# Rounding of the FFN weights moved to GpSimd, and a new order for the last two token tiles

## The reference

```python
x = x + xattn(layernorm(x), ctx, Wq, Wk, Wv, Wo)     # 16 heads of 96, 4 key/value heads, softmax in f32
x = x + ffn(layernorm(x), w_gate, w_up, w_down)      # inner width 2752

def fake_quant(t, axis):
    s = jnp.maximum(jnp.max(jnp.abs(t), axis=axis, keepdims=True) / 127.0, 1e-08)
    return jnp.clip(jnp.round(t / s), -128.0, 127.0) * s
def qlinear(x, w):                                   # per row of x, per row of w
    return jnp.einsum('bsh,oh->bso', fake_quant(x, -1), fake_quant(w, 1))
h = silu(qlinear(x, w_gate)) * qlinear(x, w_up);  out = qlinear(h, w_down)
```

## Time and profile before

| what | us |
|---|---|
| time of three runs, median (lowest to highest) | 1581.5 (1580.5 to 1582.52) |
| the profiled execution: its own time, its span | 1579.16, 1577.5 |
| busy in the span: PE, DVE, ACT, POOL | 1500.4, 1104.9, 635.1, 649.6 |
| PE's mean granted clock, share of full speed | 0.991 |

### The profile page before, as it was taken

The page is one execution under the profiler, slowest core; times in us unless marked ns, Lnnn a source line. Parts: engine busy times, 40 slices in busy tenths (PEclk is TensorE's granted clock), DMA queues, the critical chain, the costliest instruction groups (busy, mean ns, idle before and its releaser), DMA issues.

```text
span 1577.5 us, 23750 instructions
## 1 busy us (share of the span) xinstructions
PE 1500.4 (95%) x7985; PEld 747.4 (47%) x7985; DVE 1104.9 (70%) x2012; ACT 635.1 (40%) x1164; POOL 649.6 (41%) x845
## 2 busy tenths in 40 slices
PE   5999989999998999999899999979899999999997
PEld 2544445554443555444465544434444444444443
DVE  5355664666686567768576666773899999999984
ACT  4356555555454545546455545551211111111110
POOL 4187775554667654557654556671000000000000
PEclk9999999999999999999999999999999999999998
DMA  7299999879999987899998999999934233332332
GB/s 241 79 256 220 245 241 213 183 180 241 283 275 201 221 197 160 220 296 247 225 201 199 229 253 267 234 212 263 307 96 110 65 95 99 85 96 78 85 96 58
DMA packets 487084, 297.82 MB, mean 189 GB/s; under 512 B 405789, under 2 KB 443985, under 8 KB 485841
## 3 DMA queue, kind: packets, MB, share of 16 engines
q1 hardware_dynamic: 486993, 296.68, 76.0%
HBM read 143.13 MB, written 46.69 MB: 120 GB/s over the span
## 4 chain that ended last, share of the span: by engine, by line
PE 74%; SPq 8%; DMA 7%; DVE 4%; issue 2%; POOL 2%; ACT 2%; DVEq 0%; ACTq 0%
PE ps_s L1570 17%; PE ps_g L1603 10%; PE ps_g L935 10%; PE ps_g L937 10%; PE ps_g L936 10%; PE ps_s L1031 7%; SPq L807 4%; PE ps_o L1047 3%; PE ps_o L1048 3%; DMA pT<-p_nat 3%; PE ps_o L1050 2%; SPq L787 1%; DMA xnT<-xh 1%; POOL p_nat L910 1%; PE ps_s L1032 1%
## 5 line engine op out<-in xcount | busy, mean ns | idle before, releaser
L910 POOL TENSOR_TENSOR p_nat<-p_f,p_nat 128x512 f16<-128x512 f32 x256 | 309.4, 1209 | 140.8 <-ACT p_nat L1147 140.3
L905 POOL TENSOR_SCALAR p_f<-p_f,small 128x576 f32<-128x576 f32 x256 | 201.8, 788 | 273.9 <-DVE small L1261 272.9
L1136 ACT ACTIVATE p_f<-ps_s,small 128x576 f32<-128x576 f32 x256 | 188.6, 737 | 257.4 <-DVE small L1256 252.7
L1256 DVE TENSOR_REDUCE small<-ps_s 128x1 f32<-128x576 f32 x256 | 191.4, 748 | 101.8 <-PE ps_s L1032 100.7
L1031 PE MATMUL ps_s<-k,q 96*128 96x512 f16 x768 | 224.6, 382 | 22.2 <-ACT p_f L1136 19.1
L1570 PE MATMUL ps_s<-w_gu_sb,xT 128*128 128x512 bf16 (+1 forms) x1152 | 226.5, 357 | 5.4 <-DVE g_sb L1690 4.1
L1623 ACT ACTIVATE g_sb<-g_sb,sx 128x512 f32<-128x512 f32 (+1 forms) x128 | 74.5, 582 | 381.1 <-DVE g_sb L1690 331.6
L1147 ACT ACTIVATE p_nat<-p_f 128x576 f16<-128x576 f32 x256 | 172.7, 676 | 111.2 <-POOL p_f L905 60.6
L1555 POOL TENSOR_TENSOR rstd<-var_eps,minus_half 128x1 f32<-128x1 f32 x16 | 8.8, 548 | 425.1 <-DVE var_eps L1645 425.1
L1603 PE MATMUL ps_g<-w_dn_sb,hT 128*128 128x512 bf16 x704 | 162.4, 384 | 6.1 <-DMA hT<-h_int 5.3
L1570 PEld LDWEIGHTS ps_s<-w_gu_sb,xT 128*128 128x128 bf16 x1152 | 112.3, 98 | 117.2 <-DVE g_sb L1690 8.8
(11 more groups left out here) (114 smaller groups left out, 2465.9 us busy)
## 6 DMA issues: line engine op xcount, KB each, us to landing
w_in<-w_gu SPq DMA_DIRECT2D x40, 512.0 KB, 4.8
wq<-wq_c SPq DMA_DIRECT2D x36, 512.0 KB, 4.8
wo<-wo_c SPq DMA_DIRECT2D x24, 768.0 KB, 6.2
gu_q<-w_t SPq DMA_DIRECT2D x44, 256.0 KB, 4.7
w_in<-w_dn SPq DMA_DIRECT2D x8, 1376.0 KB, 7.1
x_acc<-x SPq DMA_DIRECT2D x4, 2048.0 KB, 9.0
x<-x_acc SPq DMA_DIRECT2D x8, 1024.0 KB, 6.0
x_ln<-x SPq DMA_DIRECT2D x16, 512.0 KB, 3.6
```

The costliest lines, as they stand in the source:

```text
L905: nc.gpsimd.tensor_scalar(f, f, inv_sum[:, j % 2, t:t + 1], P_UP, ALU.mult, ALU.mult).then_inc(p_scaled, 1)
L910: nc.gpsimd.tensor_tensor(h[:, S + C:2 * S], f[:, 0:T], h[:, 0:T], ALU.subtract)
L1136: nc.scalar.activation(p_f[:, tile(b, j, t) % NF, :], scores(t), ACT.Exp, bias=neg_max[:, j % 2, t:t + 1], accum_out=sums[:, j % 2, t:t + ...
L1256: nc.vector.tensor_reduce(neg_max[:, j % 2, t:t + 1], scores(t), AX.X, ALU.max, negate=True).then_inc(mx_done, 1)
```

## The change

`round` goes from DVE's stream to POOL's, with the same waits and the same due time; `turn` stays on DVE. POOL's planned order is otherwise that of before. In the FFN, `x_quant` of the next tile runs before the two products of quarter 2 instead of behind the quarter's maximum. The last tiles are written out: PE runs gates(14), the first half of down(13), gates(15), the second half of down(13), down(14), down(15). The transposed x of tile 15 goes to `xT0`, the transposed h of tiles 14 and 15 to two buffers in the part of `w_first` that held the first quarter's gate weights (free after the third group of gates(15)), and the residual of tile 14 to `x_ln`. down(15) has three pieces of 512, 256 and 256 columns, each with a bank, a result and a store of its own.

```diff
@@ stage_events
-            dve += [(t, "round", g, h), (t + 2.5, "turn", g, h)]
+            pool.append((t, "round", g, h))
+            dve.append((t + 2.5, "turn", g, h))
@@ gpsimd (the same function is removed from vector, where it waited on dve)
+        def round_off(g, h):
+            n = ITEM["w", g]
+            rows, cols = unit_part(g, h)
+            pool.wait_ge(w_up, lifts(g, h))
+            pool.wait_ge(w_turned, TURNS.index((g, h)))
+            nc.gpsimd.tensor_scalar(w_int[0:rows, 0:cols.stop - cols.start], slot_of(n)[0:rows, cols], MAGIC, None,
+                                    ALU.subtract).then_inc(w_out, 1)
@@ ffn_phase
+    hT_last = [w_first[:, i * IC * P:(i + 1) * IC * P].rearrange("p (c n) -> p c n", c=IC) for i in range(2)]
+    LAST = TILES - 1
+    PIECES_OUT = ((0, 512), (512, 256), (768, 256))
@@ x_transpose
+            other = isinstance(t, int) and t in (0, LAST)
+            if other and t:
+                sp.wait_ge(gu_done, NUSE)
+            elif not first:
                 sp.wait_ge(gu_done, t * NUSE)
...
+            sp.dma_start_transpose((xT0 if other else xT)[:], x_int[:]).then_inc(x_turned, EV)
@@ h_transpose(t, last=None)
             sp.wait_ge(h_q, t + 1)
+            if last is None:
+                sp.wait_ge(d_done, t * 2)
+            else:
+                sp.wait_ge(gu_done, LAST * NUSE + QU)
@@ sync
-        x_transpose(TILES - 1)
-        for t in (TILES - 2, TILES - 1):
-            h_transpose(t)
-            store(t - 1)
-            res_tile(t)
-        store(TILES - 1)
+        x_transpose(LAST)
+        h_transpose(LAST - 1, 0)
+        res_before_last()
+        h_transpose(LAST, 1)
+        store(LAST - 2)
+        res_tile(LAST, LAST - 1)
+        store(LAST - 1, x_ln)
+        store_last()
@@ tensor
+        def down_last():
+            pe.wait_ge(h_turned, TILES * EV)
+            for i, (a, n) in enumerate(PIECES_OUT):
+                if i < 2:
+                    pe.wait_ge(d_read, LAST * 2 + (i + 1))
+                for c in range(IC):
+                    rows = P if c < IC - 1 else I_LAST
+                    mm = nc.tensor.matmul(kept.ps_g[i][:, 0:n], hT_last[1][0:rows, c, :],
...
+                mm.then_inc(d_done, 1)
...
-        with pe.Fori(0, TILES - 2) as t:
+        with pe.Fori(0, TILES - 4) as t:
             gates(t + 2)
             down(t + 1)
-        down(TILES - 1)
+        gates(LAST - 1)
+        down(LAST - 2, halves=(0,))
+        gates(LAST, xT0)
+        down(LAST - 2, halves=(1,))
+        down(LAST - 1, False, hT_last[0])
+        down_last()
@@ vector, gates
                 gate_piece(t, q, 0)
                 gate_piece(t, q, 1)
+                if nxt is not None and q == 2:
+                    x_quant(nxt, turned)
                 product(t, q, 0)
                 product(t, q, 1)
                 quarter_max(t, q)
@@ vector, the end
+        gates(LAST - 1, LAST, LAST * EV)
+        h_part(LAST - 1, LAST * EV - EV)
+        next_x_scale()
+        result(LAST - 2, (0,))
+        gates(LAST)
+        h_part(LAST, LAST * EV, sh_last)
+        result(LAST - 2, (1,))
         next_h_scale()
+        result(LAST - 1, x_res=x_ln)
+        result_last()
```

More of the change, by code:

```diff
@@ L336, in stage_events @@
         done[n] = t
-    return act, dve, sp
+    return act, dve, pool, sp
 def token_events(b):
@@ L911, in chances_lo @@
             nc.gpsimd.tensor_tensor(h[:, S:S + C], f[:, T:S], h[:, T:S], ALU.subtract).then_inc(p_low, 1)
-        run = {"power": power, "tokens_lo": tokens_lo, "context_lo": context_lo, "scaled": chances_scaled, "low": chances_lo,
+        def round_off(g, h):
[5 more added lines that the diff above has]
+                                    ALU.subtract).then_inc(w_out, 1)
+        run = {"round": round_off, "power": power, "tokens_lo": tokens_lo, "context_lo": context_lo, "scaled": chances_scaled, "low": chances_lo,
                **ffn["gpsimd"](pool)}
@@ L1291, in tile_scale @@
             nc.vector.reciprocal(w_inv[0:rows, :], s).then_inc(w_small, 1)
[L1293 to L1300, removed]
         def turn(g, h):
@@ L1327, in vector @@
         run = {"split": w_split, "stats": norm_stats, "norm": norm_tokens, "evac": evac, "max": row_max,
-               "invert": invert, "out_lo": out_lo, "scale": tile_scale, "round": round_off, "turn": turn, "add": add_out,
+               "invert": invert, "out_lo": out_lo, "scale": tile_scale, "turn": turn, "add": add_out,
                **ffn["vector"](dve)}
@@ L1474, in x_transpose @@
             sp.nop(nofuse=True)
-            sp.dma_start_transpose((xT0 if first and t == 0 else xT)[:], x_int[:]).then_inc(x_turned, EV)
+            sp.dma_start_transpose((xT0 if other else xT)[:], x_int[:]).then_inc(x_turned, EV)
         def load_gates(q, i):
@@ L1514, in sync, with store, res_before_last, store_last @@
         ln_tile, res_tile, x_transpose = steps["ln_tile"], steps["res_tile"], steps["x_transpose"]
-        def store(t):
+        def store(t, res=x_res):
             sp.wait_ge(r_done, t * 2 + 4)
-            sp.dma_start(out[bass.ds(t * P, P), :], x_res[:]).then_inc(out_s, EV)
-        def h_transpose(t):
+            sp.dma_start(out[bass.ds(t * P, P), :], res[:]).then_inc(out_s, EV)
+        def res_before_last():
+            sp.wait_ge(x_q, TILES + 1)
+            sp.dma_start(x_ln[:], x2[(LAST - 1) * P:LAST * P, :]).then_inc(res_in, EV)
+        def store_last():
+            for i, (a, n) in enumerate(PIECES_OUT):
+                c = slice(a, a + n)
+                sp.wait_ge(r_done, LAST * 2 + 3 + i)
+                sp.dma_start(out[LAST * P:TILES * P, c], x_res[:, c]).then_inc(out_s, EV)
+        def h_transpose(t, last=None):
             sp.wait_ge(h_q, t + 1)
-            sp.wait_ge(d_done, t * 2)
+            if last is None:
+                sp.wait_ge(d_done, t * 2)
+            else:
+                sp.wait_ge(gu_done, LAST * NUSE + QU)
             sp.nop(nofuse=True)
-            sp.dma_start_transpose(hT[:], h_int[:]).then_inc(h_turned, EV)
+            sp.dma_start_transpose((hT if last is None else hT_last[last])[:], h_int[:]).then_inc(h_turned, EV)
         def load_down(q):
@@ L1587, in tensor, with gates, down @@
         first_gate = tensor_steps(pe)
-        def gates(t):
+        def gates(t, x=xT):
             pe.wait_ge(x_turned, t * EV + EV)
             for n in range(NUSE):
-                gate_group(pe, t, n, xT)
-        def down(t, first=False):
+                gate_group(pe, t, n, x)
+        def down_last():
+            pe.wait_ge(h_turned, TILES * EV)
+            for i, (a, n) in enumerate(PIECES_OUT):
+                if i < 2:
[3 more added lines that the diff above has]
+                    mm = nc.tensor.matmul(kept.ps_g[i][:, 0:n], hT_last[1][0:rows, c, :],
+                                          w_dn[0:rows, c // KC, a // 32:(a + n) // 32,
+                                               c % KC * 32:(c % KC + 1) * 32],
+                                          start=(c == 0), stop=(c == IC - 1))
+                mm.then_inc(d_done, 1)
+        def down(t, first=False, hT=hT, halves=(0, 1)):
             pe.wait_ge(h_turned, t * EV + EV)
-            for h in range(2):
+            for h in halves:
                 pe.wait_ge(d_read, t * 2 + (h + 1))
@@ L1691, in gate_piece @@
                 dve.wait_ge(gu_done, t * NUSE + (n + 2))
-                if q == 0 and not (isinstance(t, int) and t == 0):
+                if q == 0 and isinstance(t, int) and t == LAST:
+                    dve.wait_ge(r_done, t * 2 - 1)
+                elif q == 0 and not (isinstance(t, int) and t == 0):
                     dve.wait_ge(r_done, t * 2)
@@ L1732, in gates, with h_part @@
                         x_norm(nxt)
-                    elif q == 2:
-                        x_quant(nxt, turned)
-        def h_part(t, turned=None):
+        def h_part(t, turned=None, sh_next=sh_next):
             s = t * NH
@@ L1757, in next_h_scale, with result_last, result @@
             nc.vector.tensor_copy(sh[:], sh_next[:]).then_inc(sh_set, 1)
-        def result(t):
+        def result_last():
+            dve.wait_ge(h_small, LAST * NH + 16)
+            dve.wait_ge(res_in, TILES * EV)
+            for i, (a, n) in enumerate(PIECES_OUT):
+                c, u = slice(a, a + n), u_sb[:].rearrange("p h c -> p (h c)")[:, a:a + n]
+                dve.wait_ge(d_done, LAST * 2 + (i + 1))
+                nc.vector.scalar_tensor_tensor(u, kept.ps_g[i][:, 0:n], sh_last[:], s_dn[:, c], ALU.mult,
+                                               ALU.mult).then_inc(d_read, 1)
+                dve.wait_ge(d_read, LAST * 2 + (i + 3))
+                nc.vector.tensor_tensor(x_res[:, c], u, x_res[:, c], ALU.add).then_inc(r_done, 1)
+        def result(t, halves=(0, 1), x_res=x_res):
             dve.wait_ge(sh_set, t + 1)
-            for h in range(2):
+            for h in halves:
                 c = slice(h * 512, (h + 1) * 512)
```

(7 more changed lines are left out.)

13 lines of the change are left out of this document (6 added, 7 removed).

## The result

The changed kernel takes 1605.95 us (median of 5 runs, 1600.8 to 1608.17) against 1581.76 us before (1580.5 to 1582.93): 24.2 us slower, a ratio of 1.0154 with a 95% interval of 1.0131 to 1.0177. The forecast was 1574 us, faster, within 1565 to 1583; the kernel became slower, so the direction was wrong. The profiled execution took 1608.17 us, its span is 1606.4.

The account below looks back on a forecast made before the run. PE was taken as the bound, so gains lie only where it stands or is slow. The end's 5.15 + 3.04 + 0.5 + 0.3 = 9.0 us gain, less 1.5 lost in attention, took 1581.5 to 1574 us; range 1565 to 1583.

Parts of the forecast that it names:

- the price of a round: Rounding on POOL in attention: 1.14 to 1.32 us per 1024 columns, 73 to 87 us in all, 80 taken.
- 16 exposed rounds: In attention, about 16 of 60 rounds fall where PE stands still; one in four reaches PE at 1 us: 4 us lost.
- rival (b): Attention: the turn waits for POOL, POOL for the softmax; loss from 9.0 us, bound 16; chance 0.11 to 12.2 us, 0.06 beyond.
- Rival (a): Attention: DVE's shorter chain brings scores earlier, gaining 3 to 8 us, 1564.5 to 1569.5 us; chance 0.15.
- the 2.3 us of rounds on the chain: Attention: the few rounds and lengthened POOL subtractions on the chain, about 2.3 us together, gained by moving the rounding.
- The holding: Attention: DVE's rounds slow POOL's operations beside them; at up to 0.5 us for each of 60, 30 us goes.
- The end: Last FFN tiles: four terms, from the stall before down(15) to the last store, gain 9.0 us.
- Terms 1 and 2: Before and in down(15): the 5.15 us stall for the transposition of h goes, and the 3.04 us slow start.
- Term 3: After the last matmul: DVE's work is on 256 columns instead of 512, gaining 0.5 us, bounds 0 and 0.72.
- Term 4: The last store, 3.1 us: a quarter of the bytes saves between 0 and 1 us, 0.3 taken.
- The cover for x of tile 15: Before gates(15): transposed x lands at 1520.9, 0.4 us early; without the earlier `x_quant` it would be 1.4 us late.
- Rival (c): Before down(15): h of tile 15 arrives late, stall and slow clock return; a full return gives 1582 us; chance 0.06.

Follow-up runs that it names:

- the fast price: The changed kernel with the round's subtraction replaced by a mult, mult pair, integers lost, waits and places unchanged: 1573.64 us, ratio 0.9945.
- the end alone: The changed kernel with `round` back on DVE in its old place, so only the new end: 1573.36 us, ratio 0.9942.

## Why the prediction was wrong

**The first failed step** is the price of a round: "On POOL the nearest row is its one-input operation on 576 columns, 745 ns median: in proportion, 1.32 us for 1024 columns". It is 2773 ns, and 181 us in all instead of the 80 taken and the 73 to 87 of the bounds. The row was of another pair of operations, and nothing in the trace before showed POOL with this one. The bounds were drawn through one form, and so did not bound the other; the two-input row (1209 ns at 512 columns) lay nearer to the truth, 2.4 us in proportion, and should have been the upper end. With the price as assumed, the total holds to 1 us: 1573.64 measured, 1574 forecast.

The Trainium skill spoke against the move ("GPSIMD Engine Reference", section 8): VectorE is about twice as fast for elementwise work. The trace goes further: 2773 against 798 ns, 3.5 times. For mult, mult on POOL (1118 ns) against the same 798 it would be 1.4 times.

**The second failed step** is the effect on PE: one in four of 16 exposed rounds, at 1 us each, 4 us. By that rule rounds of 2.8 us would have given 11 us of loss, and a kernel of about 1581 us. Attention lost 31.4 us when only the rounding was moved. What happened is rival (b), beyond its bound of 1588.5: the turn waits for POOL, 95.9 us in 45 places, where "over 20 us" was named as the sign. Some 12 to 14 us of the loss are POOL's occupancy and 16 to 20 the late release; the two are measured by differences of kernels, and where they meet in one place, as at 1069.51, they are not told apart. The loss can be divided a second way, by what PE does: about a third, 11.2 of 33.8 us, is PE's lower clock behind its stands, for which the prediction had a term at the end and none in attention. The stretches that I took for safe were not: PE also loses 8 us in the busy one from 770 to 1020. A round of 2.8 us is probably longer than the slack there; that was not tested.

**Rival (a)**, a gain of 3 to 8 us from DVE's relief, did not show: at the fast price the time stays where it was. What relief gave there and what POOL's 68 us took were not told apart, and the 2.3 us of rounds on the chain are less than these runs can resolve.

**The holding** of POOL by DVE's round was real and smaller: L905, L910 and L911 fall by 16, 33 and 21 ns against before; times 256 that is 18 us instead of 30. The end alone, where DVE still rounds, keeps the old means (789, 1202 and 367 ns).

**The end** was right. Its chain in the changed kernel, as in the earlier trace rows:

```profile
1554.59 4.85 PE ps_g L1641 x22
1559.44 18.69 PE ps_s L1594 x96
1578.13 14.77 PE ps_g L1641 x66
1592.90 10.19 PE ps_g L1627 x66
```

The two halves of down(13), down(14) and down(15) run without a gap (14.77 us is the second half and down(14)). In the trace the end gives 9.2 us, where 9.0 were forecast. Terms 1 and 2 hold: the stall is gone, and down(15) runs at full clock. It takes 10.19 us and not 9.82: 44 matmuls of 256 columns need 0.3 to 0.4 us more than 22 of 512 (9.93 us with two pieces), which the sum had at nothing. Term 3 holds: from the last matmul to the end of DVE's work it takes 0.97 us instead of 1.50, a gain of 0.5. Term 4 was 0.8 us and not 0.3, for the last store takes 2.3 us instead of 3.1; but with two pieces, and twice the bytes in the last store, it takes 2.4 (from 1568.87 to 1571.3), so the smaller piece is not the reason, and the reason is open. All in all, three pieces give 0.4 us against two, where 0.8 was summed. The cover for x of tile 15 was at least 1.4 us too cautious: it was worked out with the DMA time of a larger transposition (5.15 us, where 4.1 was enough), and with the old `x_quant` x was complete 0.76 us after the end of gates(14) and not 1.17. The move of `x_quant` was not needed. In the time of the kernel, the end gives 7.5 us by the medians and 9.2 by the ratio, whose interval is 5.8 to 12.3.

**Rival (c)** did not happen. It let the slow clock return from about 5 us of standing; in the trace before it is there behind less. PE stood for 3.08 us up to 769.74, and from 770 to 773.3 the granted clock is 0.58.

The best version run is the end alone, 1573.4 us, faster than both kernels; its variants with two pieces and with the old `x_quant` are as fast within the noise.

## What to carry to other kernels

Price a moved operation by a row of the same engine with the same operations, not only the same number of inputs and type; if there is none, measure it alone before anything is built on it, and take the dearest neighbour as the bound. Work that goes to an engine with idle time can still cost: 60 rounds of 1.1 us cost nothing measurable, 30 of 3.0 us cost 12 us. The likely reason is that one piece is longer than the slack in front of the next urgent one. When a producer moves to a slower engine, its consumer's place in the order has to move too, for an in-order engine that waits holds everything behind it. Here that alone was worth 11 to 12 us, but only with the last pieces left early, for which the next phase waits. And a stand of PE can be paid twice, by itself and by the slower clock behind it.

## What the runs showed of the hardware

On GpSimd a `tensor_scalar` of 1024 f32 columns takes 1.05 to 1.12 us as mult, mult, with immediates or per-partition operands, but 2.77 to 2.84 us with one operation (even a single mult), and 3.6 to 3.8 us with any other pair tried; a single mult by a per-partition operand (2841 ns) is made 2.5 times as fast by a second mult by 1.0 (1118 ns). f32, f16 and bf16 outputs of the single subtraction cost the same. A conversion alone takes 1.04 us, and a subtraction of two tensors, 2.34 us, is cheaper than that of one constant.

TensorE's granted clock was low behind stands of quite different length: behind 3.08 us it was 0.58 on average for the next 3.3 us (kernel before, from 770), behind 5.58 us it was at the level of 1.2 GHz, 0.50 and 0.51, until 1083.3 (changed kernel, from 1077.7).
